# The product of exponentials and values in two visits of two key blocks instead of four of one

## The reference, cut to what matters

```
qkv    = x @ c_attn_w + c_attn_b                  # 16 heads of 8 features
scores = q @ k^T / sqrt(8), causal mask
attn   = softmax(scores)                          # heads 0 to 2 weigh one third of the keys by 1.6
out    = (attn @ v) @ c_proj_w + c_proj_b
x1     = layernorm(x + out)
h      = relu(s0 * [x1, -x1] @ (+-1)) * 2         # 128 -> 512
h      = relu(s1 * h @ (+-1)) * 2                 # 512 -> 512
y      = layernorm(x1 + s2 * h @ (+-1))           # 512 -> 128
```

## Time and profile before

| what | value |
|---|---|
| median of 3 runs | 944.77 us (943.12 to 948.06) |
| the profiled execution: its own time / its span | 946.07 us / 944.3 us |
| granted clock of PE, mean over the span | 0.944 |
| PE busy | 837.2 us (89%), 5696 matmuls |
| PE weight loads | 428.1 us (45%) |
| DVE busy | 619.5 us (66%) |
| ACT busy | 607.8 us (64%) |
| POOL busy | 523.4 us (55%) |
| value products, L901 | 2048 matmuls, 189.9 us |

### The profile page before, as it was taken

The page is one execution under the profiler, slowest core; times in us unless marked ns, Lnnn a source line. Parts: engine busy times, 40 slices in busy tenths (PEclk is TensorE's granted clock), DMA queues, the critical chain, the costliest instruction groups (busy, mean ns, idle before and its releaser), DMA issues.

```text
span 944.3 us, 17048 instructions
## 1 busy us (share of the span) xinstructions
PE 837.2 (89%) x5696; PEld 428.1 (45%) x5696; DVE 619.5 (66%) x2606; ACT 607.8 (64%) x1090; POOL 523.4 (55%) x760
## 2 busy tenths in 40 slices
PE   3257869999999999999999999999999999999855
PEld 1113324545555454545455454545454554544434
DVE  3274848595867768585958677685859586874032
ACT  3104647676777767777777767686776767686823
POOL 1102426575675757575756758575757667484741
PEclk9556979999999999999999999999999999999967
DMA  3655443536354654636363645546363636300000
GB/s 77 66 66 78 53 74 42 69 44 82 42 76 50 75 64 54 76 48 78 46 81 44 76 50 74 63 52 78 46 81 45 76 39 76 40 24 14 12 11 11
DMA packets 66284, 53.16 MB, mean 56 GB/s; under 512 B 4534, under 2 KB 64150, under 8 KB 66198
## 3 DMA queue, kind: packets, MB, share of 16 engines
q1 hardware_dynamic: 65334, 51.30, 43.5%
q10 hardware_dynamic: 864, 0.79, 0.3%
HBM read 9.24 MB, written 4.19 MB: 14 GB/s over the span
## 4 chain that ended last, share of the span: by engine, by line
PE 49%; DVE 12%; ACT 12%; DMA 11%; issue 7%; POOL 6%; SPq 2%; ACTq 0%; POOLq 0%; DVEq 0%
PE av_ps L901 9%; DMA stack<-rowmaxT 8%; PE max_ps L842 8%; PE score_ps L866 7%; PE bank_ps L928 6%; DVE max_ps L681 5%; PE bank_ps L929 5%; ACT e L556 5%; PE bank_ps L825 4%; PE bank_ps L974 3%; POOL res L472 3%; ACT full L548 3%; ACT h_hi L569 3%; DMA stack<-parts 2%; POOL rstd L464 2%
## 5 line engine op out<-in xcount | busy, mean ns | idle before, releaser
L681 DVE CUSTOM_DVE_ANT_0 max_ps<-max_ps,future 128x512 f32<-128x512 f32 (+3 forms) x1024 | 477.8, 517 | 245.4 <-PE max_ps L842 243.1
L556 ACT ACTIVATE e<-score_ps 128x512 f32<-128x512 f32 x640 | 371.0, 613 | 271.0 <-PE score_ps L866 268.9
L842 PE MATMUL max_ps<-stack 72*128 72x512 bf16 (+3 forms) x1024 | 247.7, 312 | 25.6 <-DMA stack<-parts 19.1
L866 PE MATMUL score_ps<-stack 75*128 75x512 bf16 (+3 forms) x1024 | 243.9, 302 | 28.9 <-DMA stack<-rowmaxT 20.9
L436 POOL TENSOR_SCALAR_AFFINE_SELECT e<-e 128x512 f32<-128x512 f32 x256 | 160.1, 637 | 175.7 <-ACT e L556 175.5
L444 POOL TENSOR_TENSOR h_lo<-full,h_hi 128x512 fp32r<-128x512 f32 x120 | 152.8, 1278 | 90.8 <-ACT full L548 90.8
L901 PE MATMUL av_ps<-e,vaug 128*25 128x512 f32 (+3 forms) x2048 | 189.9, 443 | 0.0
L842 PEld LDWEIGHTS max_ps<-stack 72*128 72x128 bf16 x1024 | 81.2, 99 | 160.0 <-issue 81.0
L681 DVE DVE_READ_ACCUMULATOR2_ANT rowmax<- 128x1 f32 x1024 | 143.5, 140 | 0.0
L866 PEld LDWEIGHTS score_ps<-stack 75*128 75x128 bf16 x1024 | 90.9, 98 | 107.7 <-ACT e L556 36.7
L928 PE MATMUL bank_ps<-h_hi,w 128*128 128x512 f32 x256 | 109.3, 427 | 0.2 <-ACT full L548 0.2
(11 more groups left out here) (85 smaller groups left out, 717.3 us busy)
## 6 DMA issues: line engine op xcount, KB each, us to landing
stack<-parts SPq DMA_DIRECT2D x288, 128.0 KB
x_in<-in_L_attn_hidden_states SPq DMA_DIRECT2D x16, 256.0 KB, 16.2
x_res<-in_L_attn_hidden_states SPq DMA_DIRECT2D x16, 256.0 KB, 6.2
out_x<-res SPq DMA_DIRECT2D x16, 256.0 KB, 6.8
stack<-rowmaxT ACTq DMA_DIRECT2D x32, 24.0 KB
e<-in_L_ffn_k SPq DMA_DIRECT2D x1, 256.0 KB, 3.1
e<-in_L_attn_c_attn_w SPq DMA_DIRECT2D x1, 128.0 KB
e<-in_L_ffn_k SPq DMA_DIRECT2D x1, 128.0 KB, 3.0
```

Of the source, the lines that this page charges most:

```text
L556: nc.scalar.activation(e[g % 2][:, t, :], score_ps[:, t % 2, :], ACT.Exp, scale=SCALE).then_inc(exped, 1)
L681: return nc.vector.tensor_tensor_reduce(out=scored_block, in0=scored_block, in1=future[:, P * (T - 1 - qt):S], scale=1.0, scalar=NEG, op0= ...
L842: return nc.tensor.matmul(out_ap[:, col:col + width], st[0:QK_ROWS, h, 0, P * qt:P * qt + P], st[0:QK_ROWS, h, 1, 0:width], start=True, st ...
L866: return nc.tensor.matmul(out_ap[:, col:col + width], st[0:ALL_ROWS, h, 1, P * kt:P * kt + P], st[0:ALL_ROWS, h, 0, P * kt:S], start=True, ...
```

## The change

`SUM_STEPS` gives the step at which each of the four key blocks is issued. It was 1, 3, 5, 7 and becomes 3, 3, 7, 7. The loop of `iteration` on PE is rewritten so that one step can issue two key blocks, one straight behind the other. The order of the key blocks, the waits of each, the accumulation and every other instruction stay as they are. So key block 0 moves from step 1 to step 3, ahead of key block 1, and key block 3 from step 5 to step 7, ahead of key block 2.

```diff
-SUM_STEPS = (1, 3, 5, 7)
+SUM_STEPS = (3, 3, 7, 7)
 SUMS_OUT = 8
...
                         if live(n):
                             scores(n, g, t)
-                        if t in SUM_STEPS:
-                            order = SUM_STEPS.index(t)
-                            kt = (0, 1, 3, 2)[order]
+                        for order, kt in enumerate((0, 1, 3, 2)):
+                            if SUM_STEPS[order] != t:
+                                continue
                             if g == 0 and live(n + -1):
                                 sums(n + -1, 3, kt, order)
                             if g > 0 and live(n):
                                 sums(n, g - 1, kt, order)
                         fill(n, g, t)
```

## The result

The changed kernel takes 973.27 us (median of 6 runs, 964.93 to 975.36) against 945.05 us of the kernel before (median of 6): a ratio of 1.0271, 95% interval 1.0234 to 1.0309. It is slower, as forecast, but by 28 us in place of 12, and outside the range of 948 to 963. The ratios and intervals in this document are estimates that leave out executions more than 1.5% above the fastest of their kernel (one of e3, one of e15), so they are not the quotients of the medians, which hold all of them. The profiled execution took 964.93 us, so it is at the fast end of its kernel, 19 us above the profiled execution of before.

The account below looks back on a forecast made before the run. The prediction took a chain changing hands between PE, other engines and transfers as the bound, despite PE being 89% busy. Period terms 0.63 + 0.19 + 0.13 = +0.95 us gave +11.8 in all: 957 us, range 948 to 963.

Parts of the forecast that it names:

- The size of a visit: L901 on PE: 512 + 384 columns last about 1.64 us, 128 + 256 about 0.78; a merge saves 0.22.
- Group 1: `tok_1` at (1,2) starts no earlier, so the visit leaving (1,1) makes the hole 1.08 us longer; +0.63 a period.
- Group 0: At (0,1) and (0,5) PE waits for banks that ACT frees, losing part of the saving; +0.19 us a period.
- Groups 2 and 3: PE from (1,9) to (0,0): `x1T` at (2,5) and the score tile of (3,6) keep their releasers; +0.13 us a period.
- the transfer: Row maxima land before (0,0) when the transfer backlog is through; earlier delay passes on fully, landing moves by 0.13 us.
- rival (c): The wait at (0,0), mean 0.53 us, swallows the delay: +0.42 a period, about 950 us; chance 0.07.
- Rival (b): Landing of the row maxima hangs on their issue, moving 0.28 us a period: +1.8 us, 959; chance 0.08.
- Check 4: PE's wait for POOL's L472 before `x1T` grows by about 0.5 us.
- The sum at full clock: +0.95 us a whole period, twelve of them +11.4; with the other iterations +11.8.
- rival (f): Lower clock from PE idling 1.5 us at (1,2): 10 us at 1.2 GHz, 967 us and above; chance 0.03.
- (d): No change: the hole at (1,2) doesn't grow because DVE's run starts earlier; 943 us, chance 0.07.
- (e): Faster: PE's list is the bound and all merges pay, 917 us, or 930 with two groups paying; chance 0.07.

Follow-up runs that it names:

- e3: Changed kernel with steps 3, 3, 7, 7 in step group 1 alone, 1, 3, 5, 7 in the others; 958.43 us, ratio 1.0114.
- e15: The changed kernel itself, run again beside two versions with the hole filled; 970.36 us, ratio 1.0252 against the kernel before.
- e7: Changed kernel with steps 3, 4, 5, 7: key block 0 moved to step 3 but nothing merged; 979.00 us, ratio 1.0341.
- e10: Kernel before with `x_res` issued before the nine transfers, and steps 1, 3, 7, 7 in step group 1; 938.04 us, ratio 0.9914.
- e4: Changed kernel with steps 3, 3, 7, 7 in groups 0, 2 and 3, and 1, 3, 5, 7 in group 1; 955.17 us, ratio 1.0092.
- e9: Kernel before (steps 1, 3, 5, 7) with SP issuing `x_res` before the nine transfers; 940.51 us, ratio 0.9953.
- e6: Changed kernel with steps 1, 1, 5, 5: same double visits at the first step of each pair; 961.72 us, ratio 1.0161.
- e2: Changed kernel with steps 1, 3, 7, 7: only the second pair merged, in all groups; 947.02 us, ratio 1.0025.
- e13: Changed kernel with score matmuls at (1,1) and (1,2) repeated three times, only in iterations 2 to 14; 961.86 us, ratio 1.0172.
- e12: Changed kernel with score matmuls at (1,1) and (1,2) repeated three times, also in iterations 0 and 1; 964.08 us, ratio 1.0203.
- e11: The changed kernel once more, beside a version with the hole filled; 962.43 us, ratio 1.0186 against the kernel before.
- e1: Changed kernel with steps 3, 3, 5, 7: only the first pair merged, in all groups; 964.44 us, ratio 1.0204.
- e14: Changed kernel with one repeat of the score matmuls at (1,1) and (1,2), in iterations 2 to 14; 962.21 us, ratio 1.0176.
- e8: Changed kernel with steps 1, 1, 5, 5 and SP issuing `x_res` before the nine transfers; 957.51 us, ratio 1.0116.

## Why the prediction was wrong, point by point

**The size of a visit: right.** A double visit of 512 and 384 columns lasts 1.637 us and one of 128 and 256 lasts 0.784, against 1.64 and 0.78; a merge saves 0.22 (e7).

**Group 1: right in kind, +0.77 for +0.63.** The hole grew by the whole 1.08 that the visit had taken, in two parts, since `tok_0` also met a bank that DVE (L777) was still reading. The prediction had PE's wait for L703 growing to about 1.3; the two waits together are 16.2 us in 13 periods, 1.25 each. The late pair gave less back than 0.44 - 0.21: `proj` at (1,6) now starts 0.1 later behind ACT's read-out of `attnT`, and e10 found -0.11 in place of -0.22.

**Group 0: right.** +0.26 for +0.19 (e4), with the waits of L928 and L943 for ACT's read-outs in the rows above.

**Groups 2 and 3, and the transfer: right in what mattered.** The second stretch is 23.83 for 23.92 on the mean where +0.13 was forecast. Its shortest, in periods without a wait at (0,0), went from 23.50 to 23.59, near the forecast for PE's own list; the mean wait at (0,0) shrank from 0.41 to 0.23 (the prediction had 0.53 for it, which the starts don't give). So a small part of what rival (c) said is there, 0.2 of its 0.42 a period, but the delay before (1,9) is passed on nearly in full: the first stretch grew by 1.0 and the second shrank by 0.1. That the backlog of transfers holds the landing is shown by e9, which moved one transfer and took the wait away. Rival (b), landing hangs on the issue, wanted the second stretch 0.28 longer, and it isn't.

**Check 4 failed, at no cost.** The wait for L472 before `x1T` did not grow (0.40 for 0.43): PE meets a wait for ACT at (2,2) once the visit of (2,1) is gone, and comes later than I had it. `x1T` itself came 0.13 nearer to (1,9), forecast 0.12.

**The sum at full clock: nearly right.** Twelve periods grew by 0.91 each, 10.9 us for 11.4. Iteration 1 was mis-sized: +0.1 was forecast, it went from 49.29 to 52.14, 52.45 and 53.06 in the three profiles. Part of it runs at the low clock: 4.2 us before, 9.3, 11.1 and 10.5 after. e6, which has double visits as well but only 5.0 us at the low clock there, takes 50.14, and e2, with 15.3 us, takes 53.55, so most of the excess goes with the clock. Of the 18.7 us by which the profiled span grew, 17.1 are iterations 2 to 13 (10.9 and four falls), 2.3 lie before iteration 2, 0.7 are iteration 14, as forecast, and behind it 1.4 were gained. With iteration 1 as measured, the changed kernel without a fall is at 960, the fastest of its executions (959.99), where 957 was forecast.

**The clock: the step that failed.** I gave rival (f) 0.03, because all windows of before showed 1.00, and wrote that PE would idle "1.5 us in one piece at (1,2) where it idled 0.4". But those windows were of a kernel that idled 0.4 us there, so they said nothing of the longer hole, and the sum has no term for the clock. The clock fell in some iterations, to 1.2 GHz for 3.4 us, from which a period loses 1.6 us. On the chip of e15 the hole costs 5 to 8 us of the median. The 13 us between 960 and 973 in the first comparison are only argued to be the clock: the profiled execution (964.93 us, 0.939) has four falls, and of the slower ones three (973.07 to 975.36 us) have a mean granted clock of 0.928 to 0.933 and one (973.84) has 0.963. A high mean of this kind stands beside an ordinary time in the kernel before, too (946.49 us at 0.976, 946.61 at 0.944), so the mean clock is a hint and not a count of falls. In that comparison the hole was not filled, and none of the slower executions was profiled. Rival (f) had the place and the direction right; its price was reckoned from 10 us at 1.2 GHz, while each fall lasts 3.4 us and comes back in later periods, so that its 967 and above met the median partly by luck. Rivals (d) and (e) are out: the releasers stayed where they were.

## What to carry to other kernels

Before a block of work on the busiest engine is moved or merged, ask of the place that it leaves what the engine would wait for there. Where the answer is another engine's chain, the block was free there and is paid at its new place. Here the saving of 0.22 us a merge was real, and moving 1.08 us out of a 0.4 us hole cost four times that; only where the leaving place had no cover to lose (the late pair of group 1) was a merge a gain. And a hole on PE is not only its own length: behind 1.5 us of it in two pieces the clock was down for the next work in some periods, so that filling the hole with useless matmuls made this kernel 5 to 8 us faster on one chip (e13 against e15). On another, where the fill also ran in iterations 0 and 1, it gained nothing (e12 against e11), and against the kernel before both lose. A window of a trace that shows full clock says so for the idling that it holds, not for a longer one.

## What the runs showed of the hardware that was not expected

- The granted clock of PE fell to 1.2 GHz for 3.4 us behind a stretch of 3.9 us in which PE was busy for 2.86, and back to 2.4 GHz. It did so in 13 of 36 equal periods, often in successive ones: iterations 10 to 13, and 3 to 6 with 9 to 11. The same instructions with the same waits in the other periods had full clock. Executions of one kernel then spread over 15 us (964.27 to 979.47), where e9 spreads over 1.8 (939.89 to 941.70). Not all spread is this: e10 has no fall between 130 and 880 us in its profile and spreads over 10 (931.62 to 942.12).
- With a third of the fill, 0.22 us each at (1,1) and (1,2), the profile has no fall at (1,2). That this is enough isn't shown: e1 has the whole hole and no fall in its profile either, and one of e14's executions took 967.06 us at a mean clock of 0.934.
- Falls came at other places too: at (2,8) in e6 and e8 behind a wait of 0.79 us for ACT, and at (2,3) in 3 of 48 periods with the fill.
- A small load on ACT's queue (24 KB) landed 2.7 us after its issue with little else moving, and 5.1 to 7.5 us after it while the nine transfers, `x_res` and the output were under way (iterations 2 to 13 of the kernel before), most often 0.7 to 1.5 us after the last of the nine. Issuing `x_res` earlier took that wait off the path.
